# A Mamba layer and a SwiGLU layer on one core: states kept in sliding regions, and the relu part of softplus added by an accumulating transfer

## The reference

```python
x_in, res = split(x @ W_in)
u     = silu(causal_conv4(x_in) + conv_b)
dt, B, C = split(u @ W_x)                     # ranks 16, 16, 16
delta = softplus(dt @ W_dt + b_dt)            # [tokens, 512]
h[t]  = exp(delta[t] * A) * h[t-1] + delta[t] * u[t] * B[t]   # per channel and state
y[t]  = sum over states of h[t] * C[t]  + u[t] * D
x1 = layernorm(x + (y * silu(res)) @ W_out)
out = layernorm(x1 + (silu(x1 @ Wg.T) * (x1 @ Wu.T)) @ Wd.T)
```

## Time and profile before

| | |
|---|---|
| time, median of 3 runs | 1819.03 us (1818.59 to 1819.52) |
| profiled execution, span from first to last instruction | 1814.1 us |
| what lies around the span, median less span | 4.9 us |
| busy: DVE, PE, POOL, ACT | 1703.6, 1687.1, 1635.8, 1610.8 us |
| POOL's products with B, 1024 | 1306.7 us |
| DVE's scans, 960 and 64 | 1185.6 and 94.7 us |

### The profile page before, as it was taken

The page is one execution under the profiler, slowest core; times in us unless marked ns, Lnnn a source line. Parts: engine busy times, 40 slices in busy tenths (PEclk is TensorE's granted clock), DMA queues, the critical chain, the costliest instruction groups (busy, mean ns, idle before and its releaser), DMA issues.

```text
span 1814.1 us, 32557 instructions
## 1 busy us (share of the span) xinstructions
PE 1687.1 (93%) x10128; PEld 1264.6 (70%) x10128; DVE 1703.6 (94%) x1958; ACT 1610.8 (89%) x2769; POOL 1635.8 (90%) x1629
## 2 busy tenths in 40 slices
PE   8879899999999999899999999999899999998788
PEld 3556676776767677676776767677676776867667
DVE  4999999999999999999999999999999999999994
ACT  4888989899898998989899898998989899898874
POOL 2989899998989989899998989989899998989970
PEclk9999999999999999999999999999999999999999
DMA  7323123222222223223222322323223232221110
GB/s 245 114 71 116 49 82 114 74 106 83 105 82 83 105 94 117 71 82 117 71 107 81 105 83 82 107 93 117 71 83 117 71 110 78 105 72 58 36 47 25
DMA packets 82108, 164.57 MB, mean 91 GB/s; under 512 B 10369, under 2 KB 28033, under 8 KB 81938
## 3 DMA queue, kind: packets, MB, share of 16 engines
q1 hardware_dynamic: 80498, 160.90, 25.2%
q10 hardware_dynamic: 1440, 1.58, 0.3%
HBM read 87.47 MB, written 8.91 MB: 53 GB/s over the span
## 4 chain that ended last, share of the span: by engine, by line
PE 70%; ACT 16%; POOL 6%; issue 5%; DVE 3%; DMA 0%; DVEq 0%; SPq 0%; ACTq 0%; POOLq 0%
PE ht_upper L737 10%; PE ht_lower L737 10%; PE y_upper L762 9%; PE fill L559 8%; PE fill L673 8%; PE fill L663 7%; PE fill L642 5%; POOL dbu L1237 4%; PE fill L574 3%; ACT da_ahead L1094 2%; ACT L1167 2%; PE fill L612 2%; ACT gt L1103 2%; ACT L1179 2%; ACT kb L993 2%
## 5 line engine op out<-in xcount | busy, mean ns | idle before, releaser
L1237 POOL TENSOR_TENSOR dbu<-du,brep 128x512 f32<-128x512 f32 x1024 | 1306.7, 1306 | 122.2 <-DVE h L1432 96.1
L1432 DVE TENSOR_TENSOR_SCAN h<-da,carry,dbu 128x512 f32<-128x512 f32 x960 | 1185.6, 1269 | 45.8 <-ACT da L1094 43.1
L1094 ACT ACTIVATE da<-delta,a_s 128x512 f32<-128x512 f32 x960 | 660.4, 694 | 62.7 <-DVE h L1432 59.4
L1103 ACT ACTIVATE gt<-ht_upper,ct 128x512 f32<-128x512 f32 x512 | 350.5, 685 | 71.3 <-PE ht_upper L737 67.3
L737 PEld LDWEIGHTS ht_upper<-ident,h 128*128 128x128 f32 x2048 | 241.8, 141 | 195.6 <-issue 122.2
L737 PE MATMUL ht_upper<-ident,h 128*128 128x128 f32 x2048 | 312.7, 275 | 70.2 <-ACT gt L1103 53.3
L1444 DVE SCALAR_TENSOR_TENSOR acc<-ht_lower,ct,acc 128x512 f32<-128x512 f32 x480 | 350.9, 731 | 4.0 <-PE ht_lower L737 2.5
L737 PE MATMUL ht_lower<-ident,h 128*128 128x128 f32 x2048 | 312.6, 275 | 25.9 <-DVE acc L1444 21.8
L737 PEld LDWEIGHTS ht_lower<-ident,h 128*128 128x128 f32 x2048 | 239.5, 141 | 102.5 <-DVE h L1432 53.4
L762 PE MATMUL y_upper<-ident,gt 128*128 128x128 f32 x2048 | 308.2, 273 | 0.0
L762 PEld LDWEIGHTS y_upper<-ident,gt 128*128 128x128 f32 x2048 | 245.0, 141 | 43.7 <-issue 31.3
(11 more groups left out here) (189 smaller groups left out, 1868.1 us busy)
## 6 DMA issues: line engine op xcount, KB each, us to landing
brep<-b_rows SPq DMA_DIRECT2D x127, 512.0 KB, 3.7
xs<-xin SPq DMA_DIRECT2D x242, 256.0 KB, 2.5
xr<-x SPq DMA_DIRECT2D x16, 512.0 KB, 4.0
xt_s<-x_t SPq DMA_DIRECT2D x15, 512.0 KB, 3.7
out<-xr SPq DMA_DIRECT2D x15, 512.0 KB, 2.9
win_s<-w_in SPq DMA_DIRECT2D x2, 512.0 KB, 5.1
h<-xin SPq DMA_DIRECT2D x4, 256.0 KB, 4.2
h<-xin ACTq DMA_DIRECT2D x4, 256.0 KB, 4.6
```

What stands on the lines that cost most here:

```text
L1094: nc.scalar.activation(dst[:, :], delta[:, par, m, :], ACT.Exp, scale=a_s[:, m, n:n + 1])\
L1103: nc.scalar.activation(gt[:, (n * UPPER + k) % GT, :], ht_upper[:, :], ACT.Copy, scale=ct[:, par, k, n:n + 1])\
L1237: nc.gpsimd.tensor_tensor(dbu[:, beat % DBU, :], du[:, par, m, :], brep[:, n // PIECE % 2, n % PIECE, :], ALU.mult).then_inc(dbu_ready, 1)
L1432: nc.vector.tensor_tensor_scan(h[:, n % 2, m, 0:T], da[beat % 2][:, :] if slot is None else da_ahead[:, slot, :], dbu[:, beat % DBU, :], c ...
```

## The change

`h` gets T + 31 columns instead of T + 1. Each state's region starts one column earlier than that of the state before it in the same buffer, over 32 places in the four chunks of a sequence, so that the last column of each state is not written over before the next chunk's scan of that state, which takes its start value there. Carry copies, the carry tile, the zero column and their semaphores are gone; a new sequence starts from the constant zero. The scan now waits for the scan of the same beat one chunk earlier.

The add of the relu part becomes a transfer issued from POOL's queue, of 128 partitions x 2 KB, that accumulates `du` into `delta`. It has a semaphore for each block, for which the product with u and the first exponentials of the next chunk wait. The beats of these steps are set anew.

```diff
-BEAT = {"soft exp": [48.5, 51, 56.5, 56.5], "soft ln": [49, 51.5, 57, 59.5], "add u": [52, 55, 60, 63],
-        "times u": [53, 56, 63, 63], ...
+BEAT = {"soft exp": [48.5, 51, 55.5, 56], "soft ln": [49, 51.5, 57, 58.5], "add u": [52, 55, 58, 60],
+        "times u": [55, 58, 62, 63], ...
...
+    SLIDE = PER_SEQ * NS // 2 - 1
...
-        h = sb("h", [P, 2, DB, T + 1])
-        carry = sb("carry", [P, NS, DB])
+        h = sb("h", [P, 2, DB, T + SLIDE])
...
+        def h_at(c, n):
+            return SLIDE - (c % PER_SEQ * (NS // 2) + n // 2)
+        def h_times(c, n, m, first, last):
+            return h[:, n % 2, m, h_at(c, n) + first:h_at(c, n) + last]
+        def h_end(c, n, m):
+            return h_times(c, n, m, T - 1, T)
...
             def exp(i, par, beat):
-                if n == 0:
-                    act.wait_ge(delta_ready, i * DB + m + 1)
+                if n == 0 and i:
+                    act.wait_ge(delta_added[m], 16 * i)
+                elif n == 0:
+                    act.wait_ge(delta_ready, m + 1)
...
             def positive_part(c, par, m):
                 pool.wait_ge(relu_ready, (c - 1) * DB + m + 1)
                 pool.wait_ge(dt_ln, c * DB + m + 1)
-                nc.gpsimd.tensor_tensor(delta[:, par, m, :], delta[:, par, m, :], du[:, par, m, :], ALU.add)\
-                    .then_inc(delta_ready, 1)
+                pool.dma_start(delta[:, par, m, :], du[:, par, m, :], accum_op=ALU.add).then_inc(delta_added[m], 16)
             def times_u(c, par, m):
-                pool.wait_ge(delta_ready, c * DB + m + 1)
+                pool.wait_ge(delta_added[m], 16 * c)
...
-            def save_carry(i, n, ends):
-                start = T - 1 + ends
-                nc.gpsimd.tensor_copy(carry[:, n, :], h[:, n % 2, :, start])\
-                    .then_inc(carry_saved, 1)
...
-            nc.gpsimd.memset(h[:, :, :, T:T + 1], 0.0).then_inc(zeros_set, 1)
...
-                after(dve, carry_saved, i * NS + n - 1)
-                nc.vector.tensor_tensor_scan(h[:, n % 2, m, 0:T], ...,
-                                             carry[:, n, m:m + 1], ALU.mult, ALU.add).then_inc(h_ready, 1)
+                begins = i % PER_SEQ == 0
+                if not begins:
+                    dve.wait_ge(h_ready, (i - 1) * NH + beat + 1)
+                nc.vector.tensor_tensor_scan(h_times(i, n, m, 0, T), ...,
+                                             0.0 if begins else h_end(i - 1, n, m),
+                                             ALU.mult, ALU.add).then_inc(h_ready, 1)
```

More of the change, by code:

```diff
@@ L65 @@
            "down2": 61.5, "down3": 63}
-BEAT = {"soft exp": [48.5, 51, 56.5, 56.5], "soft ln": [49, 51.5, 57, 59.5], "add u": [52, 55, 60, 63],
-        "times u": [53, 56, 63, 63], "x1 cut": [29, 35], "x1 low": [30.5, 31.5], "y upper": [5.5, 6.5],
+BEAT = {"soft exp": [48.5, 51, 55.5, 56], "soft ln": [49, 51.5, 57, 58.5], "add u": [52, 55, 58, 60],
+        "times u": [55, 58, 62, 63], "x1 cut": [29, 35], "x1 low": [30.5, 31.5], "y upper": [5.5, 6.5],
         "times z": [8, 11, 13, 17], "mean": [21, 64], "rstd": [22, 79], "shift": [24, 90],
@@ L93 @@
             if start < at % 64 <= end]
-SAVE_AT = 3
 assert all(b - a > AHEAD + 1 for a, b in zip(SILUS, SILUS[1:]))
@@ L260, in mamba_swiglu @@
         acc_begun, acc_done = sem("acc_begun"), sem("acc_done")
-        carry_saved, zeros_set = sem("carry_saved"), sem("zeros_set")
         first_loaded = [sem(f"first_loaded{m}") for m in range(DB)]
@@ L273, in mamba_swiglu @@
         relu_ready = sem("relu_ready")
+        delta_added = [sem(f"delta_added{m}") for m in range(DB)]
         delta_ready, du_ready, b_written = sem("delta_ready"), sem("du_ready"), sem("b_written")
@@ L733, in fill, with turn @@
                                 fill_back(i - 1, name, part)
-            def turn(bank, n, t):
+            def turn(bank, i, n, t):
                 for m in range(DB):
-                    mm = nc.tensor.transpose(bank[:, m * P:(m + 1) * P], h[:, n % 2, m, t * P:(t + 1) * P], ident[:, :])
+                    mm = nc.tensor.transpose(bank[:, m * P:(m + 1) * P], h_times(i, n, m, t * P, (t + 1) * P), ident[:, :])
                 return mm
@@ L742, in turn_upper @@
                 after(pe, gt_ready, i * NUP + n * UPPER + k)
-                turn(ht_upper, n, k).then_inc(upper_turned, 1)
+                turn(ht_upper, i, n, k).then_inc(upper_turned, 1)
             def turn_lower(i, n, k):
@@ L752, in turn_lower @@
                     after(pe, acc_done, i * NSUM + max(before - LOWER + 1, 0))
-                turn(ht_lower, n, UPPER + k).then_inc(lower_turned, 1)
+                turn(ht_lower, i, n, UPPER + k).then_inc(lower_turned, 1)
             def turn_back(i, par, n, k):
@@ L798, in _ @@
             pe.wait_ge(small_loaded, 16 * 7)
-            pe.wait_ge(tiles_set, 5)
+            pe.wait_ge(tiles_set, 4)
             pe.wait_ge(diag_ready, DB)
@@ L1126, in _ @@
             act.wait_ge(conv_loaded, 32)
-            act.wait_ge(tiles_set, 5)
+            act.wait_ge(tiles_set, 4)
             copy(xin[:, :, 0:HALO], xin[:, :, T:T + HALO]).then_inc(xin_ready, 1)
@@ L1289, in times_z @@
                     .then_inc(upper_done if k < DP else lower_done, 1)
-            def save_carry(i, n, ends):
-                start = T - 1 + ends
-                nc.gpsimd.tensor_copy(carry[:, n, :], h[:, n % 2, :, start])\
-                    .then_inc(carry_saved, 1)
             def step(i, par):
                 first, last = [isinstance(i, int) and i == c for c in (0, NCH - 1)]
-                ends, ended = [int(c % PER_SEQ == PER_SEQ - 1) for c in (i, i - 1)]
                 for beat in range(NH):
@@ L1304, in step @@
                         cast(*divmod((beat - CAST_AT) // 2, 3))
[L1305 to L1309, removed]
                     for which in [] if first else tiles_due("shift", beat):
@@ L1324, in step @@
                         times_u(i + 1, 1 - par, m)
-            nc.gpsimd.memset(h[:, :, :, T:T + 1], 0.0).then_inc(zeros_set, 1)
-            pool.wait_ge(zeros_set, 1)
             steps(step)
@@ L1429, in scan @@
                 after(dve, lower_turned, i * NLOW + (n - 1) * LOWER)
-                after(dve, carry_saved, i * NS + n - 1)
-                nc.vector.tensor_tensor_scan(h[:, n % 2, m, 0:T], da[beat % 2][:, :] if slot is None
+                begins = i % PER_SEQ == 0
+                if not begins:
+                    dve.wait_ge(h_ready, (i - 1) * NH + beat + 1)
+                nc.vector.tensor_tensor_scan(h_times(i, n, m, 0, T), da[beat % 2][:, :] if slot is None
                                              else da_ahead[:, slot, :], dbu[:, beat % DBU, :],
-                                             carry[:, n, m:m + 1], ALU.mult, ALU.add).then_inc(h_ready, 1)
+                                             0.0 if begins else h_end(i - 1, n, m),
+                                             ALU.mult, ALU.add).then_inc(h_ready, 1)
             def sum_states(i, par, n, k):
@@ L1455, in _ @@
             nc.vector.memset(wdt_s[:, :], 0.0).then_inc(wdt_zero, 1)
-            nc.vector.memset(carry[:, :, :], 0.0).then_inc(tiles_set, 1)
             nc.vector.memset(xin[:, :, T:T + 2 * HALO], 0.0).then_inc(tiles_set, 1)
@@ L1470, in _ @@
             dve.wait_ge(res2_done, TT)
-            dve.wait_ge(tiles_set, 5)
+            dve.wait_ge(tiles_set, 4)
             dve.wait_ge(ident_ready, 1)
```

## The result

The changed kernel takes 1827.17 us (median of 4 runs, 1824.25 to 1827.87), the kernel before 1819.03 beside it (median of 3 runs; a fourth took 9732.87 us and is left out, with it the median is 1819.28). The ratio is 1.0045, 95% interval 1.0033 to 1.0057: slower by 8 us, where 9 were forecast. The profiled execution has a span of 1825.6 us and a time of its own of 1827.4, so 1.8 us lie around the span. The 4.9 us that I put around the span of the kernel before were therefore most likely not all around it: that execution was some 3 us shorter than its median.

The account below looks back on a forecast made before the run. The ring DVE, PE, ACT was taken as the bound, POOL mattering once its lead is spent. 14 x 0.60 = 8.4 plus 0.8 in step 0 made 9.2, so 1819.0 + 9.2 = 1828 us, range 1816.5 to 1846.

Parts of the forecast that it names:

- What bounds the kernel: Four engines almost level in a 108.7 us step; the ring goes DVE, PE, ACT, DVE, with POOL running ahead.
- the lead of POOL: POOL's product is ready 3.0 us before scan 63, but only 0.45 us before scan 0 of the next chunk.
- Issue 2 waits for the logarithm at beat 58: POOL's transfer issue for block 2 waits for ACT's logarithm, 0.68 us later than it could, later products queued behind.
- 2I - 1.50 us a step: DVE's lateness from POOL's products at beats 59 to 63; 0.60 us a step with I = 1.05.
- I: Time one accumulating transfer's issue takes in POOL's queue; taken as 1.05 us, forecast case 0.75 to 1.5.
- Step 0: First chunk's step: product 0 ready at 144.0 instead of 143.25, a loss of 0.8 us.
- The sliding regions: cost and gain nothing: Removed carry copies free 2.3 us of POOL a step, covered by POOL's lead; h's longer rows leave times unchanged.
- The sum: 14 x 0.60 = 8.4 us for steps 1 to 14, 0.8 for step 0, 0 for step 15: 9.2 us.
- Softplus beats and landing: 0: Earlier logarithms make no scan late, and transfers land within the 6.0 us or more before their u-products: 0.
- The cheap issue: Rival: POOL's issue takes up to 0.75 us, DVE is nowhere late, 1818 to 1819 us; chance 33 in 100.
- The dear one: Rival: issue or landing is dear, 1835 us at I = 1.28, some 1860 at 2.0; 15 in 100 for over 1840.
- The faster DVE at scan 32: Rival: POOL's product holds scan 32 0.2 us instead of 1.1, 0.9 a step, 1806 us; chance 7 in 100.

Follow-up runs that it names:

- experiment 1: The changed kernel with adds on POOL and the beats of before, so only the sliding regions: 1813.96 us, ratio to before 0.998.
- experiment 4: The changed kernel with only the issue for block 2 moved from beat 58 to 59, behind product 59: 1813.63 us, ratio to before 0.998.
- experiment 5: The changed kernel with only ACT's logarithm of block 2 moved from beat 57 to 55.5: 1814.09 us, ratio to before 0.9982.
- experiment 2: The changed kernel with its new beats, but POOL does the four adds itself instead of issuing transfers: 1830.59 us, ratio to before 1.0068.
- plain issue: The changed kernel with plain transfers in place of the accumulating ones, losing the logarithm's part of softplus: 1816.79 us in one run.
- experiment 8: The sliding regions alone, but scans that begin a sequence take zero from a one-column tile instead of the constant: 1817.19 us, ratio to before 0.9991.
- experiment 9: The sliding regions alone, but POOL still makes carry copies, except in the last chunk, which no scan reads: 1816.99 us, ratio to before 0.9995.
- experiment 3: The changed kernel with the transfers but the beats of before for adds and products with u: 1947.03 us, ratio to before 1.0709.

## Why the prediction was right, point by point

*What bounds the kernel; the lead of POOL.* Right. Four nearly level engines, POOL ahead by 3.0 us at beat 63, and the loss fell where that lead was spent, from scan 59 to scan 0, in every step but the last. Experiments 1, 4 and 5 show the bound once more: three different kernels, one with adds on POOL and two with transfers, all take 1813.6 to 1814.1 us. As long as POOL keeps its lead, what it does costs and gives nothing.

*Issue 2 waits for the logarithm at beat 58.* Shown, from both sides of the wait (experiments 4 and 5), and shown not to be the transfer's doing (experiment 2).

*2I - 1.50 us a step.* The form holds; both terms in it were off and cancelled in part. The wait ends 0.50 us later than I had it, since 0.56 us pass between the end of ACT's logarithm and the issue, where I had allowed 0.06. And I, from the issue to a result behind it, is 0.60 + 0.30 = 0.90, where I had 1.05. That makes 2 x 0.90 - 1.50 + 0.50 = 0.80 us. Measured over steps 1 to 14, against before: 0.74 a step, 10.4 us in all, where 8.4 were forecast. The cleaner comparison is with the kernels of experiments 4 and 5, which differ by one number and share the shorter scans: 0.77 and 0.82 a step. The same form fits the other two kernels that keep the order. With the adds on POOL, I is 1.23 and the add starts 0.14 us after the logarithm instead of 0.06: 2.46 - 1.50 + 0.08 = 1.04; measured against experiment 1, 1.03. With the plain issue, I is 0.60: 1.20 - 1.50 + 0.50 = 0.20; measured against 4 and 5, 0.10 and 0.15.

*Step 0.* Wrong in sign: +0.8 forecast, 109.5 to 109.0 measured in the two profiled executions. The stall itself is there and larger than forecast, 1.5 to 1.9 us against the 107.5 and 107.1 of experiments 5 and 4. I had taken the rest of the step as unchanged, but it got shorter (107.4 us in experiment 1). Its 64 scans start from a constant and take 0.06 us less, and the copies are gone; experiments 8 and 9 leave open which of the two did it.

*The sliding regions: cost and gain nothing.* Wrong by about 4 us, which experiment 1 gains over before. So the loss made by POOL's queue is larger than forecast: by the ratios the kernel after is 12 us slower than those of experiments 4 and 5, not 9.2. The measured 8 are some 12 lost and some 4 gained. That the sum came within about 1 us is in this part luck: a loss put too low and a gain left out.

*The sum.* Between the two profiled executions the difference is made up of +10.4 in steps 1 to 14, -0.5 in step 0, and +1.5 in the last step and behind it (106.1 to 107.2, and 43.1 to 43.4), which is the 11.5 us between the two spans. The last step has nothing of the change's order in it and took 105.8 to 108.5 us in the kernels of experiments 1, 4 and 5, so I take its share as scatter. The medians differ by 8 because the profiled execution of before was some 3 us shorter than its median.

*Softplus beats and landing: 0.* Right. No scan is late for an exponential that stands behind a logarithm, and u-products wait for no landing. The 6.0 us that I allowed from issue 3 to its u-product were 5.5, and block 3's transfers landed in 4.8 at most. The slowest landing of all, 5.9, is of block 1, which has 7.8 us. The least that any product with u had to spare was 0.7 us. I had taken one landing time for all four; experiment 3 shows what a transfer of SP's beside them does to it, and what it costs where there is no room.

*The rivals.* The cheap issue (I up to 0.75) did not come about: even the plain one leaves DVE waiting for POOL once a step (3.0 us in 11 times), since my limit of 0.75 left out the 0.50 us between the logarithm's end and the issue. It gives nearly that rival's time, though, 1816.8 in its one run. The dear one is refuted by the 0.90 and by the landings. The faster DVE at scan 32: two scans take 3.13 us there instead of 3.36, not the 2.6 that I expected, and DVE waits the longer behind them; a mean over steps 2 to 14 gives 1.7 us of idle before scan 34. In the rows of step 7, of DVE and then of POOL:

```profile
850.85 3.13 DVE L1431 TENSOR_TENSOR_SCAN h<-da_ahead,h,dbu 128x512 f32<-128x512 f32 x2
```
```profile
845.52 6.20 POOL L1250 TENSOR_TENSOR dbu<-du,brep 128x512 f32<-128x512 f32 x5
852.88 2.17 POOL L1250 TENSOR_TENSOR dbu<-du,brep 128x512 f32<-128x512 f32 x1 [1.16 <-DVE h L1431]
```

The rule of the Trainium skill, "SBUF — State Buffer", section "Who interferes with whom", is still borne out by the 3.13 us, and from the other side by POOL's product that starts beside scan 33 and takes 2.17 us instead of 1.28. Scans 44 and 45 also have both inputs in SBUF, but POOL stands idle beside them, and they take 1.28 and 1.26 us; scan 32 alone takes 1.95. But the product ahead was hardly moved out of the way: it ends 0.87 us after scan 32's start (851.72 against 850.85), where it was 1.11 before. The Trainium skill, "DMA: Bandwidth & Descriptors", section "Latency and other measured facts", puts about 1 us to the first byte on this path; the first packets at 1.16 us (plain) and 1.46 us (accumulating) agree roughly, the first better than the second.

## What to carry to other kernels

Where several engines are level, look for the engine with a lead, and add up along its queue what an edit puts ahead of the instruction that the bound engine wants next, each semaphore of another engine included; a wait there costs even where the work removed is larger. Try the wait from both sides, by moving the waiting instruction behind what it holds up and by moving what it waits for. A transfer in place of a compute instruction needs distance, and what else is issued near it counts: here 3.3 us pass from issue to landing when it is alone and 5.6 to 7.5 when 512 KB are issued beside it. With a single instruction between issue and use in three of four places, the kernel was 7% slower.

## What the runs showed of the hardware that was not expected

- An accumulating transfer of 256 KB between SBUF tiles, issued by GpSimd, takes 0.89 us of issue, lands in 3.3 us where nothing else is near, and uses 8640 packets for 60 of them; a plain one 0.58 us, 2.3 us and 4800. Their first packets start 1.46 and 1.16 us after the issue. With a 512 KB transfer issued by SP within 0.4 us they land in 5.6 to 7.5 and in 4.5 to 4.9 us.
- The instruction behind either starts 0.60 us after the issue's start, if it has nothing else to wait for. Behind an accumulating one, POOL's results come 0.30 us later (1.28 us without one, 1.57 behind one issue, 1.86 behind two), until POOL idles. Behind a plain one they don't. Why is not shown.
- From the end of ACT's logarithm to the issue that waited for it, 0.55 us pass, in all 15 steps that have one. The same holds for the first issue of each step, whose logarithm ends while POOL is still busy, so the 0.55 us are not a matter of POOL standing idle. To an add in the issue's place 0.14 us pass; from POOL's product to DVE's scan 0.08 (899.97 to 900.05).
- DVE's scan of 128x512 takes 1211 ns from a constant, 1270 from a column of a tile. The product that POOL starts beside scan 33, whose two inputs are both in SBUF, takes 2.11 to 2.18 us in the 16 steps instead of 1.28, and scan 32 beside POOL's product 1.95 in step 7 where scans 44 and 45, with POOL idle, take 1.28 and 1.26.
